# Loading each later head's operand stack in twelve half-length pieces, one every five tiles of keys, instead of in six transfers at once

## The chip, the cores and the metric

The kernel runs on one core of a Trainium2 chip. The metric is the device time of one execution, in microseconds; lower is better. The engines are TensorE (PE, with its weight loads PEld), VectorE (DVE), ScalarE (ACT), GpSimd (POOL) and SyncE (SP). Sixteen DMA engines move data between DRAM and the on-chip memory.

## What is computed

One block of a transformer on 4096 tokens of width 256: half a mixture-of-experts layer, attention, and half a mixture-of-experts layer again, each behind a layer norm. The part that the change touches is the attention:

```python
qkv = jnp.einsum('bsi,oi->bso', x, w_qkv)            # S = 4096 tokens, 16 heads of 16
logits = jnp.einsum('bhsd,bhtd->bhst', q, k) * scale
logits = jnp.where(mask, logits, neg_inf)            # causal
probs = jax.nn.softmax(logits, axis=-1)
out = jnp.einsum('bhst,bhtd->bhsd', probs, v)
```

## The kernel before, in words

**Precision by parts.** Queries and keys are split into three bf16 parts each (the number, its rest, the rest of that). The projections are computed once, the parts are stored to `qk_parts` in DRAM, and every head reads its rows back into a *stack* of 96 partitions by 4096 tokens, once for queries (c = 0) and once for keys (c = 1): `K_PARTS = (3, 2, 1)` says that the first query part stands against three key parts, the second against two, the third against one. Two more partitions hold the row maxima of the queries. There are two stack buffers; head h uses buffer h % 2, so head h + 1 can be loaded once all transposed scores of head h - 1 are done.

**The order of the work.** `attention_steps()` is one list that all engines walk. Its steps are the *tiles* of probabilities: head by head, block of 512 queries by block (j = 0 to 7), tile of 128 keys by tile; a head has 144 tiles. Around them stand, a fixed amount of work ahead (`LEAD`), the scores that only serve to find the row maxima ("scores"), then for each block the joining of its maxima ("unit_max") and their way into the stack ("max_row"), and, up to five tiles behind, the products with the values ("pv").

- PE computes the scores for the maxima (L967 to L971), the transposed scores of a tile (L989) and the products with the values (L932). L940 is the helper that issues the score matmuls in groups of 32 columns. The first scores of the next head stand before tile 98 of this one; they are the first that wait for its stack (`stack_ready`, L914).
- ACT takes the exponential of each tile (L730).
- DVE reduces the scores to maxima (L1344) and copies the joined maxima (L1356).
- POOL zeroes what lies behind the diagonal in the last four tiles of each block (L519, the "select"), splits the joined maxima in two bf16 parts (L510, L512), and issues the stack loads (L484). It does these in the order of the list, each when its turn comes.
- SP sends the row maxima into the stack (L599), two transfers of 1 KB per block.

**The load of a stack** is `load_stack` (L474): six transfers, issued back to back: 48 partitions of queries and 48 of keys (384 KB each), 32 and 32 (256 KB each), 16 and 16 (128 KB each), every partition's row 4096 tokens or 8 KB long. The steps list places the load of head 1 before tile 6 of head 0, and that of head h + 1 before tile 24 of head h. Head 0 is loaded by SP in small blocks and is not changed; head 15 loads nothing, as there is no head 16.

Of the kernel before, what the change touches and what calls it, by code (L numbers as in the profile page):

```python
# [15 lines left out]
S = 4096  # L16
# [3 lines left out]
H = 16  # L20
HD = D // H
# [27 lines left out]
K_PARTS = (3, 2, 1)  # L49
# [12 lines left out]
PV_LAG, PV_PAUSE, FINISH_LAG = 5, 2, 3  # L62
GRID = 32
MAX_ROW_LAG = 4
FIRST_LOAD = 6

UNITS = [(h, j) for h in range(H) for j in range(NJ)]

# [6 lines left out]
PER_HEAD = ITEMS // H  # L75
# [32 lines left out]
def keys_of(j, i, k):  # L108

    if i == DIAGONAL:  # L110
        return 0, QB
    return k * QB, min(QB * j + P * i, (k + 1) * QB)


def attention_steps():

    begun, ended = EARLY_CHUNKS, EARLY_CHUNKS
    for _ in range(NEXT_CHUNKS):
        yield "begin_chunk", begun
        begun += 1  # L120
        if begun - ended > 1:
            yield "end_chunk", ended
            ended += 1
    yield "end_chunk", ended
    ended += 1
    a, a_done, b_done, u, unsent = 0, 0, 0, 0, []
    summed, pause, unfinished = 0, 0, []
    for n in range(ITEMS):
        while a < len(A_ITEMS) and a_done < b_done + LEAD:
            h, j, i, k = A_ITEMS[a]  # L130
            yield "scores", a
            lo, hi = keys_of(j, i, k)
            a_done += hi - lo
            a += 1
            if a == len(A_ITEMS) or A_ITEMS[a][:2] != (h, j):
                yield "unit_max", u
                unsent.append((a + MAX_ROW_LAG, u))
                u += 1
            while unsent and (unsent[0][0] <= a or a == len(A_ITEMS)):
                yield "max_row", unsent.pop(0)[1]  # L140
            if n == 0 and begun < len(CHUNKS):
                if begun > ended:
                    yield "end_chunk", ended
                    ended += 1
                yield "begin_chunk", begun
                begun += 1
            elif ended < begun:
                yield "end_chunk", ended
                ended += 1
        h, j, t = B_ITEMS[n]  # L150
        if n == FIRST_LOAD:
            yield "load_stack", 1
        if j == 3 and t == 0 and 1 <= h < H - 1:
            yield "load_stack", h + 1
        yield "probs", n
        b_done += QB - max(t - TPJ * j, 0) * P

        for _ in range(0 if pause else 2):
            if summed > n - PV_LAG:
                break  # L160
            yield "pv", summed
            h, j, t = B_ITEMS[summed]
            summed += 1
            if t == TPJ * (j + 1) - 1:
                yield "acc", h * NJ + j
                unfinished.append((n + FINISH_LAG, h * NJ + j))
                pause = PV_PAUSE + 1
                break
        pause = max(pause - 1, 0)
        while unfinished and unfinished[0][0] <= n:  # L170
            yield "finish", unfinished.pop(0)[1]
    while summed < ITEMS:
        yield "pv", summed
        summed += 1
    yield "acc", len(UNITS) - 1
    for _, u in unfinished:
        yield "finish", u
    yield "finish", len(UNITS) - 1
# [67 lines left out]
def macaron_block(nc, x_in, w_qkv_t, w_out_t, gate_w, gate_b, w1, w2, w3, bias_cols, out):  # L246
    with ExitStack() as ctx:
        sig = Signals(nc, ctx)
# [21 lines left out]
        parts_dram = nc.dram_tensor("qk_parts", (2, 3, D, S), BF16).ap()  # L270
# [49 lines left out]
        def carve(n):  # L320
            wat[0] += n
            assert wat[0] <= WORK
            return work[:, wat[0] - n:wat[0]]
# [15 lines left out]
        def bf(ap):  # L339
            return ap.bitcast(BF16)  # L340

        wat[0] = 0
        stack = bf(carve(2 * 2 * S // 2)).rearrange("p (b c s) -> p b c s", b=2, c=2)
# [30 lines left out]
        def _(eng):  # L374
            need = Waits(eng)
# [91 lines left out]
            def part3(n):  # L467
                b, b_f = n % SPLIT_BF, n % SPLIT_F
                need.wait_ge(sig.part2, n + 1)
                need.wait_ge(sig.parts_stored[b], 16 * (n // SPLIT_BF))  # L470
                eng.tensor_tensor(split_bf[:, b, 2], split_f[:, b_f], split_bf[:, b, 1],  # L471
                                  ALU.subtract).then_inc(sig.part3, 1)

            def load_stack(h):  # L474
                last = EARLY_CHUNKS if h < H // KD else len(CHUNKS)
                for n in range(last - SPLIT_BF, last):
                    need.wait_ge(sig.parts_stored[n % SPLIT_BF], 16 * (n // SPLIT_BF + 1))
                need.wait_ge(sig.scores_t, PER_HEAD * (h - 1))
                r = 0
                for part, count in enumerate(K_PARTS):  # L480
                    q_rows = parts_dram[0, part, h * HD:(h + 1) * HD, :].unsqueeze(0).to_broadcast([count, HD, S])
                    k_rows = parts_dram[1, 0:count, h * HD:(h + 1) * HD, :]
                    for c, src in enumerate((q_rows, k_rows)):
                        eng.dma_start(stack[r * HD:(r + count) * HD, h % 2, c, :], src).then_inc(sig.stack[h % 2], 16)  # L484
                    r += count

            def attention():
                need.wait_ge(sig.staged[0], len(STAGES))
                eng.memset(v_aug[:, :, :, HD:VW], 1.0).then_inc(sig.ones, 1)
                need.wait_ge(sig.layer[0][2], N_TILES)  # L490
                need.wait_ge(sig.weighted[0], KD * N_TILES)
                need.wait_ge(sig.v_part[0], KD * N_TILES)
                for b in range(2):
                    need.wait_ge(sig.ones, 1 + b)
                    eng.memset(stack[QK_ROWS:QK_ROWS + M_PARTS, b, 1, :], 1.0).then_inc(sig.ones, 1)
                need.wait_ge(sig.ones, 3)
                eng.memset(maxima, NEG).then_inc(sig.ones, 1)
                for n in range(EARLY_CHUNKS):
                    part3(n)
                for what, n in attention_steps():  # L500
                    if what == "end_chunk":
                        part3(n)
                    elif what == "load_stack":
                        load_stack(n)
                    elif what == "unit_max":
                        b = n % MAX_RING
                        need.wait_ge(sig.neg_max, n + 1)

                        need.wait_ge(sig.a_full, row_place[n - MAX_RING] + 1 if n >= MAX_RING else 0)
                        eng.tensor_copy(max_parts[:, b, 0], neg_max[:, b, :]).then_inc(sig.max_parts, 1)  # L510
                        need.wait_ge(sig.max_parts, 2 * n + 1)
                        eng.tensor_tensor(max_parts[:, b, 1], neg_max[:, b, :], max_parts[:, b, 0],  # L512
                                          ALU.subtract).then_inc(sig.max_parts, 1)
                    elif what == "probs":
                        h, j, t = B_ITEMS[n]
                        lo = (t - TPJ * j) * P
                        if lo >= 0:
                            need.wait_ge(sig.exp, n + 1)
                            eng.affine_select(  # L519
                                out=p_ring[:, n % P_RING, lo:lo + P], in_=p_ring[:, n % P_RING, lo:lo + P],  # L520
                                compare_op=ALU.is_ge, fill=0.0, base=0, pattern=[[1, P]], channel_multiplier=-1,
                            ).then_inc(sig.causal, 1)

            route(0)
            tiles(0)
            attention()
            route(1)
            tiles(1)
# [236 lines left out]
        def _(eng):  # L765
            need = Waits(eng)
# [147 lines left out]
            def stack_ready(h, j):  # L914
                if h == 0:
                    for sc in range(j + 1):
                        need.wait_ge(sig.first_stack[sc], 96)
                else:
                    need.wait_ge(sig.stack[h % 2], 96 * ((h + 1) // 2))

            def pv(n):

# [21 lines left out]
            def attention():  # L944
# [4 lines left out]
                for what, n in attention_steps():  # L949
# [5 lines left out]
                    elif what == "scores":  # L955
                        h, j, i, k = A_ITEMS[n]
                        lo, hi = keys_of(j, i, k)
                        place = scores_place[n]
                        out = bank[A_BANKS[place % len(A_BANKS)]]
                        stack_ready(h, j)  # L960
                        need.wait_ge(sig.a_done, place - len(A_BANKS) + 1)
                        need.wait_ge(sig.rest1, EARLY_CHUNKS)
# [474 lines left out]
```

## Time and profile before

| | us |
|---|---|
| median of three runs | 2474.4 |
| lowest, highest | 2459.2, 2475.3 |
| the profiled execution | 2466.8 |
| its span | 2465.1 |

| engine | busy us | share of the span |
|---|---|---|
| PE | 2289.1 | 93% |
| PEld | 1923.7 | 78% |
| DVE | 1915.6 | 78% |
| ACT | 1565.5 | 64% |
| POOL | 476.0 | 19% |

The attention takes the stretch from about 492 to 2078 us of the span. "issue" in a row is time in which an engine waited for nothing that the profile shows. DMA traffic is listed by queue: q0 is what POOL issues, q1 what SP issues, q8 and q14 are of the kind "instruction", which no line of the kernel issues. PEclk is the granted share of TensorE's clock: 1.00 is 2.4 GHz, 0.50 is 1.2 GHz.

### The profile page before, as it was taken

What the parts mean: (1) busy time and instruction counts of PE and PEld (TensorE: products, weight loads), DVE (VectorE), ACT (ScalarE), POOL (GpSimd) and SP (SyncE); (2) the same over time, 40 slices, a digit from 0 to 9 for tenths busy, and PEclk for the clock granted to TensorE, in tenths of its full rate; (3) what the DMA queues carried; (4) which work ended last, traced back from release to release, by engine and by line L of the source; (5) the groups of instructions that cost most, each with busy time, mean ns of one, the idle gap of its engine ahead of it and who ended that gap; (6) DMA issues with size and microseconds to landing.
All of it is one profiled execution on the core that took longest, in us unless ns stands there. A gap on an engine that the chain in (4) does not pass through costs nothing.

```text
span 2465.1 us, 97220 instructions
## 1 busy us (share of the span) xinstructions
PE 2289.1 (93%) x42097; PEld 1923.7 (78%) x42097; DVE 1915.6 (78%) x4310; ACT 1565.5 (64%) x3252; POOL 476.0 (19%) x1133
## 2 busy tenths in 40 slices
PE   6799988889999999999999999999999999779998
PEld 5588865358788888897888878888888786748886
DVE  6755544389898998898999988998989894575554
ACT  2244423448787887787888877887878786224441
POOL 1533211311110111111202101111011110043330
PEclk7799978979999999999999999999999999779997
DMA  6311102410110101101101111011010103031112
GB/s 207 91 45 48 42 1 84 138 37 4 29 19 14 29 4 29 29 4 29 20 13 29 15 17 29 4 29 29 4 29 13 20 4 105 1 106 45 49 45 68
DMA packets 78179, 96.12 MB, mean 39 GB/s; under 512 B 26868, under 2 KB 69624, under 8 KB 74872
## 3 DMA queue, kind: packets, MB, share of 16 engines
q0 software_dynamic: 24768, 44.75, 8.9%
q1 hardware_dynamic: 52016, 44.10, 5.7%
q8 instruction: 331, 5.42, 1.0%
q10 hardware_dynamic: 968, 1.06, 0.1%
q14 instruction: 96, 0.79, 0.1%
HBM read 64.14 MB, written 25.43 MB: 36 GB/s over the span
## 4 chain that ended last, share of the span: by engine, by line
PE 85%; issue 6%; DVE 5%; POOL 1%; DMA 1%; ACT 1%; ACTq 0%; POOLq 0%; DVEq 0%
PE bank L940 42%; PE bank L932 18%; PE bank L842 17%; PE bank L890 2%; PE bank L802 2%; PE bank L853 1%; DVE work L1344 1%; PE bank L1025 1%; POOL phase L471 1%; DVE work L1199 1%; PE bank L781 1%; DVE work L1202 1%; PE bank L860 1%; DMA qk_parts<-phase 0%; ACT feat L638 0%
## 5 line engine op out<-in xcount | busy, mean ns | idle before, releaser
L940 PE MATMUL bank<-work 96*32 96x512 bf16 (+6 forms) x19968 | 1484.8, 353 | 26.0 <-issue 22.2
L730 ACT ACTIVATE feat<-bank 128x512 f32<-128x512 f32 (+3 forms) x2304 | 1256.1, 565 | 312.4 <-PE bank L940 235.1
L1344 DVE TENSOR_REDUCE work<-bank 128x1 f32<-128x512 f32 (+3 forms) x2176 | 1288.9, 637 | 104.7 <-PE bank L940 90.4
L932 PE MATMUL bank<-feat,phase 128*17 128x128 f32 x16896 | 1200.2, 275 | 35.2 <-issue 35.2
L940 PEld LDWEIGHTS bank<-work 96*32 96x32 bf16 (+1 forms) x19968 | 890.0, 97 | 118.6 <-issue 30.7
L932 PEld LDWEIGHTS bank<-feat,phase 128*17 128x17 f32 x16896 | 824.0, 99 | 144.0 <-issue 41.6
L842 PE MATMUL bank<-work 128*128 128x256 f32 x1872 | 435.0, 382 | 3.5 <-issue 2.2
L842 PEld LDWEIGHTS bank<-work 128*128 128x128 f32 x1872 | 340.8, 191 | 53.8 <-issue 12.4
L519 POOL TENSOR_SCALAR_AFFINE_SELECT feat<-feat 128x128 f32<-128x128 f32 x512 | 145.6, 292 | 728.4 <-ACT feat L730 722.5
L1252 DVE COPY work<-phase 128x514 f32 x234 | 100.6, 430 | 189.7 <-ACT work L689 59.3
L458 POOL DMA_INDIRECT work<-token_table,row_no x156 | 148.7, 953 | 282.7 <-DVE work L1266 243.3
L673 ACT ACTIVATE work<-work 128x256 f32<-128x256 f32 x156 | 63.6, 408 | 181.5 <-DVE work L1273 181.5
L510 POOL CAST work<-work 128x4 bf16<-128x4 f32 x128 | 23.8, 186 | 590.3 <-DVE work L1350 590.3
L689 ACT ACTIVATE work<-bank,work 128x256 f32<-128x256 f32 x156 | 65.4, 470 | 87.4 <-PE bank L842 87.4
L1341 DVE TENSOR_REDUCE work<-bank 128x4 f32<-128x512 f32 x128 | 87.8, 686 | 11.8 <-PE bank L940 8.0
L940 PE MATMUL bank<-mask_bf,ident_bf 128*32 128x512 bf16 x512 | 87.1, 383 | 0.1
L1320 DVE TENSOR_TENSOR phase<-bank,phase 128x512 f32<-128x512 f32 x32 | 22.1, 691 | 82.3 <-ACT phase L698 75.5
L679 ACT ACTIVATE work<-bank 128x512 f32<-128x512 f32 x78 | 44.9, 576 | 60.8 <-PE bank L853 60.8
L1304 DVE TENSOR_TENSOR x_res<-x_res,bank 128x512 f32<-128x512 f32 x48 | 32.8, 688 | 57.0 <-PE bank L890 30.3
L1273 DVE SCALAR_TENSOR_TENSOR work<-bank,work 128x256 f32<-128x256 f32 x156 | 67.9, 476 | 11.2 <-PE bank L842 10.9
L940 PE MATMUL bank<-ident,work 128*32 128x68 f32 x1024 | 73.0, 225 | 0.4 <-ACT work L736 0.4
L1282 DVE TENSOR_SCALAR work<-bank,work 128x256 f32<-128x256 f32 x156 | 67.9, 478 | 1.7 <-PE bank L842 1.7
(147 smaller groups left out, 1474.9 us busy)
## 6 DMA issues: line engine op xcount, KB each, us to landing
phase<-in_w SPq DMA_DIRECT2D x12, 1024.0 KB, 12.5
qk_parts<-phase SPq DMA_DIRECT2D x32, 384.0 KB, 2.6
work<-qk_parts POOLq DMA_DIRECT2D x30, 384.0 KB, 2.8
token_table<-rows SPq DMA_DIRECT2D x8, 1056.0 KB, 8.9
work<-qk_parts POOLq DMA_DIRECT2D x30, 256.0 KB, 8.7
x_res<-in_x SPq DMA_DIRECT2D x4, 1024.0 KB, 13.5
work<-work SPq DMA_DIRECT2D x256, 1.0 KB
out<-x_res SPq DMA_DIRECT2D x4, 1024.0 KB, 4.4
```

Of the source, the lines that this page charges most:

```text
L458: eng.indirect_dma_start(out=x_slot[:, j % NXG, u, :], out_offset=None, in_=table[f], in_offset=bass.IndirectOffsetOnAxis(ap=row_no[:, n:n ...
L519: eng.affine_select(out=p_ring[:, n % P_RING, lo:lo + P], in_=p_ring[:, n % P_RING, lo:lo + P], compare_op=ALU.is_ge, fill=0.0, base=0, pa ...
L689: eng.activation(acts[:, 1, j % 2, m], bank[2][:, m * TILE:(m + 1) * TILE], ACT.Relu, bias=staged[:, j % 2, 0, KD * D + m:KD * D + m + 1], ...
L730: eng.activation(p_ring[:, n % P_RING, lo:QB], bank[bk][:, lo:QB], ACT.Exp, scale=HD ** -0.5).then_inc(sig.exp, 1)
L842: mm = eng.matmul(bank[bk][:, m * TILE:(m + 1) * TILE], staged[:, b, l, k * D + m * P:k * D + (m + 1) * P], acts[:, l, b, k], start=(k == ...
L932: mm = eng.matmul(bank[ACC_BANK][GRID * g:GRID * g + VW, 0:P], v_aug[:, t, h, :], p_ring[:, n % P_RING, g * P:(g + 1) * P], start=(t == 0) ...
L940: mm = eng.matmul(out[GRID * g:GRID * (g + 1), width], left[:, GRID * g:GRID * (g + 1)], right, start=start, stop=stop)
L1252: eng.tensor_copy(staged[:, j % 2, l, :], experts[:, bass.ds(expert, 1), l, :].rearrange("p a w -> p (a w)"),).then_inc(sig.staged[f], 1)
L1273: eng.scalar_tensor_tensor(weighted[:, j % 2, m], bank[4][:, m * TILE:(m + 1) * TILE], staged[:, j % 2, 2, KD * D + m:KD * D + m + 1], w_r ...
L1282: eng.tensor_scalar(acts[:, 2, j % 2, m], bank[3][:, m * TILE:(m + 1) * TILE], staged[:, j % 2, 1, KD * D + m:KD * D + m + 1], 0.0, ALU.ad ...
L1341: eng.tensor_reduce(maxima[:, h % 2, j, :, 0], scores[:, 0:QB].rearrange("p (i s) -> p i s", i=TPJ), AX_X, ALU.max).then_inc(sig.a_done, 1)
L1344: eng.tensor_reduce(maxima[:, h % 2, j, i, k + 1:k + 2], scores[:, 0:hi - lo], AX_X, ALU.max).then_inc(sig.a_done, 1)
```

## The change

The six transfers become twelve: each is cut into the tokens 0 to 2047 and 2048 to 4095, so a partition's row is 4 KB. The pieces stand before tiles 24, 29, 34, ... 79 of the head before, also for head 1. The wait before the first scores of a head counts twelve transfers instead of six.

```diff
-FIRST_LOAD = 6
+
+LOAD_PIECES = [(part, c, half) for part in range(len(K_PARTS)) for c in range(2) for half in range(2)]
+LOAD_FIRST, LOAD_EVERY = 24, 5
...
-        if n == FIRST_LOAD:
-            yield "load_stack", 1
-        if j == 3 and t == 0 and 1 <= h < H - 1:
-            yield "load_stack", h + 1
+        piece, between = divmod(n - PER_HEAD * h - LOAD_FIRST, LOAD_EVERY)
+        if h < H - 1 and between == 0 and 0 <= piece < len(LOAD_PIECES):
+            yield "load_stack", (h + 1, piece)
...
-                r = 0
-                for part, count in enumerate(K_PARTS):
-                    q_rows = parts_dram[0, part, h * HD:(h + 1) * HD, :].unsqueeze(0).to_broadcast([count, HD, S])
-                    k_rows = parts_dram[1, 0:count, h * HD:(h + 1) * HD, :]
-                    for c, src in enumerate((q_rows, k_rows)):
-                        eng.dma_start(stack[r * HD:(r + count) * HD, h % 2, c, :], src).then_inc(sig.stack[h % 2], 16)
-                    r += count
+                part, c, half = LOAD_PIECES[piece]
+                count, r = K_PARTS[part], sum(K_PARTS[:part])
+                tokens = slice(half * S // 2, (half + 1) * S // 2)
+                if c == 0:
+                    src = parts_dram[0, part, h * HD:(h + 1) * HD, tokens].unsqueeze(0).to_broadcast([count, HD, S // 2])
+                else:
+                    src = parts_dram[1, 0:count, h * HD:(h + 1) * HD, tokens]
+                eng.dma_start(stack[r * HD:(r + count) * HD, h % 2, c, tokens], src).then_inc(sig.stack[h % 2], 16)
...
-                    need.wait_ge(sig.stack[h % 2], 96 * ((h + 1) // 2))
+                    need.wait_ge(sig.stack[h % 2], 16 * len(LOAD_PIECES) * ((h + 1) // 2))
```

Only POOL's order changes. These are POOL's instructions over one head in the middle of the attention before; `work<-qk_parts` is a stack load, the shape its partitions and tokens, AFFINE_SELECT the select at the diagonal, CAST and TENSOR_TENSOR the splitting of a block's maxima:

```order
L519 AFFINE_SELECT feat<-feat 128x128 x6
L484 DMA work<-qk_parts 48x1x4096 x2
L484 DMA work<-qk_parts 32x1x4096 x2
L484 DMA work<-qk_parts 16x4096 x2
L510 CAST work<-work 128x4
L512 TENSOR_TENSOR work<-work 128x4
L519 AFFINE_SELECT feat<-feat 128x128 x8
L510 CAST work<-work 128x4
L512 TENSOR_TENSOR work<-work 128x4
L519 AFFINE_SELECT feat<-feat 128x128 x4
```

And the same stretch of the changed program (its lines stand two to three further down):

```order
L521 AFFINE_SELECT feat<-feat 128x128 x6
L487 DMA work<-qk_parts 48x1x2048 x3
L512 CAST work<-work 128x4
L514 TENSOR_TENSOR work<-work 128x4
L521 AFFINE_SELECT feat<-feat 128x128 x3
L487 DMA work<-qk_parts 48x1x2048
L521 AFFINE_SELECT feat<-feat 128x128
L487 DMA work<-qk_parts 32x1x2048 x3
L521 AFFINE_SELECT feat<-feat 128x128 x3
L487 DMA work<-qk_parts 32x1x2048
L521 AFFINE_SELECT feat<-feat 128x128
L487 DMA work<-qk_parts 16x2048
```

It goes on with the splitting of the next block's maxima, the last three loads (16x2048 x3), and the four selects of the following block. The twelve loads do not stand alone: three follow each other after tile 23, one and then three stand on the two sides of the select of tile 39, one and one on the two sides of the select of tile 59, and three behind the next maxima.

## Rows read from the trace of the kernel before

**Rows 1.** The page: busy time of PE, and the chain that ended last.
```profile
PE 2289.1 (93%) x42097; PEld 1923.7 (78%) x42097; DVE 1915.6 (78%) x4310; ACT 1565.5 (64%) x3252; POOL 476.0 (19%) x1133
PE 85%; issue 6%; DVE 5%; POOL 1%; DMA 1%; ACT 1%; ACTq 0%; POOLq 0%; DVEq 0%
```

**Rows 2.** Waits of PE: who, for what, us in total, times, longest us.
```profile
PE bank L932 <- issue: 35.2, 9, 5.8
PE bank L940 <- issue: 22.2, 5, 7.8
```

**Rows 3.** The chain in order of time, head 1: start us, us, what.
```profile
636.86 5.83 issue
```

**Rows 4.** DMA queues from 627.0 to 627.3 us: packets, MB, share of 16 engines.
```profile
q8 instruction: 1, 0.02, 20.0%
```

**Rows 5.** DMA queues from 627.3 to 639.8 us.
```profile
DMA packets 807, 1.08 MB, mean 87 GB/s; under 512 B 675, under 2 KB 675, under 8 KB 675
...
q0 software_dynamic: 807, 1.08, 50.0%
```

**Rows 6.** DMA queues from 639.8 to 640.1 us.
```profile
q8 instruction: 1, 0.02, 27.9%
```

**Rows 7.** DMA queues from 630.2 to 645.9 us, one whole load.
```profile
DMA packets 948, 1.62 MB, mean 103 GB/s; under 512 B 753, under 2 KB 753, under 8 KB 753
...
q0 software_dynamic: 945, 1.58, 52.1%
q8 instruction: 2, 0.03, 1.0%
```

**Rows 8.** DMA queues from 1985 to 2060 us, head 15, no load.
```profile
q8 instruction: 15, 0.25, 1.4%
```

**Rows 9.** DMA queues from 632.3 to 639.8 us, the middle of a load.
```profile
DMA packets 158, 0.92 MB, mean 122 GB/s; under 512 B 46, under 2 KB 46, under 8 KB 46
```

**Rows 10.** Stretches: busy us (instructions) by engine, then PEclk, DMA share, GB/s.
```profile
640.00:646.00 6.00, 3.31 (x55) 2.65 (x59) 1.38 (x2) 1.15 (x3) 0.58 (x2) 0.50 0.33 82
...
1319.00:1327.00 8.00, 8.00 (x227) 7.32 (x221) 7.36 (x17) 6.66 (x13) 1.51 (x6) 1.00 0.71 133
2004.00:2012.00 8.00, 8.00 (x228) 7.22 (x222) 7.36 (x16) 6.67 (x13) 1.51 (x6) 1.00 0.02 6
```

**Rows 11.** POOL in order of time at tile 24 of heads 1, 8, 9 and 15.
```profile
628.28 0.54 POOL L519 TENSOR_SCALAR_AFFINE_SELECT feat<-feat 128x128 f32<-128x128 f32 x2 [0.15 <-ACT feat L730]
628.76 3.45 POOL L484 DMA_DIRECT2D work<-qk_parts  x6
...
1315.08 3.45 POOL L484 DMA_DIRECT2D work<-qk_parts  x6
...
1407.63 3.45 POOL L484 DMA_DIRECT2D work<-qk_parts  x6
...
1999.77 0.54 POOL L519 TENSOR_SCALAR_AFFINE_SELECT feat<-feat 128x128 f32<-128x128 f32 x2 [0.15 <-ACT feat L730]
```

**Rows 12.** PE in order of time, head 0, behind the load of head 1.
```profile
531.03 0.63 PE L932 MATMUL bank<-feat,phase 128*17 128x128 f32 x8 [4.56 <-issue]
```

**Rows 13.** POOL in order of time, head 8: selects 38, 39; 57 to 59; two maxima.
```profile
1324.81 0.54 POOL L519 TENSOR_SCALAR_AFFINE_SELECT feat<-feat 128x128 f32<-128x128 f32 x2 [0.15 <-ACT feat L730]
...
1337.05 0.91 POOL L519 TENSOR_SCALAR_AFFINE_SELECT feat<-feat 128x128 f32<-128x128 f32 x3 [0.31 <-ACT feat L730]
1341.62 0.19 POOL L510 CAST work<-work 128x4 bf16<-128x4 f32 x1 [3.67 <-DVE work L1350]
...
1362.47 0.19 POOL L510 CAST work<-work 128x4 bf16<-128x4 f32 x1 [9.08 <-DVE work L1350]
```

**Rows 14.** DVE and ACT, head 8: block 5's maxima copied; its first exponential.
```profile
1326.12 0.27 DVE L1356 CAST work<-bank 8x128 bf16<-8x128 f32 x1
...
1337.76 1.25 ACT L730 ACTIVATE feat<-bank 128x512 f32<-128x512 f32 x2 [0.16 <-PE bank L940]
```

**Rows 15.** DMA queues from 392 to 465 us, rows of 1 KB, issued by SP.
```profile
q1 hardware_dynamic: 7872, 7.47, 31.1%
```

More of the change, by code:

```diff
@@ L472, in part3, with load_stack @@
                                   ALU.subtract).then_inc(sig.part3, 1)
-            def load_stack(h):
+            def load_stack(h, piece):
                 last = EARLY_CHUNKS if h < H // KD else len(CHUNKS)
@@ L503, in attention @@
                     elif what == "load_stack":
-                        load_stack(n)
+                        load_stack(*n)
                     elif what == "unit_max":
```

## The prediction

> **What bounds the kernel now.** I first read the page: PE is busy for 93% of the span and the chain that ended last lies on it for 85%, with 6% of "issue" [rows 1]. So the other engines cost nothing as long as PE is fed. Then the waits of PE: the largest are for no engine but for "issue", 35.2 + 22.2 = 57.4 us in 14 waits of up to 7.8 us [rows 2]. All fourteen lie in the attention, one in each of heads 0 to 14 but head 8. The chain shows the one of head 1: from 636.86 us on PE stands still for 5.83 us [rows 3], 8 us after POOL issued the six loads of head 2's stack at 628.76 [rows 11].
>
> What PE lacks there is told by the queue of the kind "instruction". In head 15, which loads nothing, q8 moves 15 packets in 75 us, one every 5.0 us [rows 8]. In head 1 one starts at about 627.2 [rows 4], then in 12.5 us there is none, only q0, the stack load [rows 5], and the next comes at 639.8 [rows 6]. PE stops 9.7 us after the first of them and goes on at 642.69, 2.9 us after the second. So the program's own instructions were late, behind the stack's data. From this follows the slack: PE lives 9.7 us on a packet and needs the next 2.9 us before it can go on, so a spacing of 6.8 us does no harm, and a packet may be **1.8 us** late against the usual 5.0.
>
> **What it costs now.** Heads 8 and 9 give the length of a head without such a wait: 1407.63 - 1315.08 = 92.55 us from load to load [rows 11]. From the last selects before tile 24 in head 1 (628.28) to the same in head 15 (1999.77) are 1371.5 us, for 14 heads, against 14 x 92.55 = 1295.7. So the loads of heads 1 to 14 cost 75.8 us. That is more than their 57.4 - 4.6 = 52.8 us of waiting (4.56 us is head 0's, [rows 12]), a factor of 1.44: behind the wait the granted clock is 0.50, that is 1.2 GHz [rows 10], and PE, which had stood still, works at half speed for a while. Head 0 at the same factor: 4.56 x 1.44 = 6.6 us. **All loads together: 82.4 us.** The heads with no wait show that this is all of it: head 8's PE is busy for 8.00 us of 8 with the DMA engines at 0.71, like head 15's at 0.02 [rows 10]. The stack's data do not slow PE's work, they only hold up its instructions.
>
> **The change, part by part.**
>
> *Removed: the burst of 1.57 MB.* Minus 82.4 us, if nothing takes its place.
>
> *Added: the pieces, which are not evenly spaced.* POOL issues a piece as soon as it gets to it, and waits only at selects and maxima. By its order the three pieces of tiles 24, 29 and 34 go out together after select 23 (at 1315.1 in head 8); those of tiles 39 to 54 together around select 39, ten us later (select 38 and 39 start at 1324.81); those of 59 and 64 at about 1338; the last three behind the maxima at 1341.6 [rows 13]. The first burst is 3 x 192 KB = 0.59 MB. The second is 192 + 3 x 128 KB, again 0.59 MB. The third and fourth have 0.20 MB each.
>
> *What a burst does to the instruction packets.* The load of head 2 moves 1.58 MB in 15.7 us [rows 7] and holds the packet back until 639.8, 9.6 us after the data began to flow. For a burst of 0.59 MB there are three readings. In proportion (9.6/15.7 of the time that 0.59 MB takes at 103 GB/s, 5.7 us) the hold is 3.5 us. At the rate of the load's middle, 122 GB/s [rows 9], the burst is gone after 4.8 us. At worst the packet comes with the burst's last byte at the mean rate, 5.7 us. At best packets get through and the hold is under 1.8 us. I take 4.8 us, since in a burst three transfers of nearly one size run side by side to the end, as in the middle of the load.
>
> *The residual.* A packet is due every 5.0 us, at any moment of the burst, and stalls PE by what it is late over 1.8 us. Not every packet lies in the way: a hold of 9.6 us should cost 9.6 - 2.5 - 1.8 = 5.3 us on average, and the fifteen loads cost 57.4/15 = 3.8, so 0.72 of the packets are caught. A burst with a hold T costs 0.72 x (T - 1.8)^2 / (2 x 5.0): for 4.8 us 0.65, for 3.5 us 0.21, for 5.7 us 1.1. Fifteen loads have 30 large bursts: **19 us** (6 and 33 at the ends; none at best). The two small bursts of each head are drained in 0.20 MB / 103 GB/s = 1.9 us and cost nothing. So short a wait should not lower the clock: I take no factor.
>
> The Trainium skill (DMA: Bandwidth & Descriptors, "Why a DMA increments its semaphore by 16 and not by 1") says that a transfer issued by POOL runs on the largest number of engines up to 16 that divides the slowest dimension on both sides. By it the pieces with three and two copies run on three and two engines, a large burst puts 16 packets of 4 KB on each of nine engines, and with half of the load's 0.68 us a packet (below) a packet is held 5.4 us and the residual would be an estimate of 22 us instead of 19. The trace agrees roughly: by the rule ten of sixteen engines, 0.63, carry the middle of a load, and the share there is 0.71.
>
> *POOL's own time.* Six issues take 3.45 us [rows 11], so twelve take 6.9, or 0.58 each. POOL is busy for 19% of the span and waits before nearly every select. The piece before tile 39 puts 0.6 us ahead of the select of tile 39, the one before 59 the same; the product that waits for the select stands five tiles behind, about 3 us. Nothing.
>
> *The row maxima.* SP's transfer of block 5's maxima now falls into the second burst: they are copied at 1326.12 in head 8 and first used for an exponential at 1337.76, 11.6 us later [rows 14]. A hold of 5.7 us fits. Nothing, but see the last rival.
>
> *Being in time.* The last pieces go out from 1341.6 to 1343.4 and are there by 1346; the next head's first scores come just before the maxima at 1362.5 [rows 13]. Some 16 us of slack. Head 1's load, moved from tile 6 to 24, has the same slack. More packets of half the size: by time per byte they cost the same. SP's rows of 1 KB took 0.311 x 73 x 16 / 7872 = 0.046 us each [rows 15], the stack's packets of 8 KB (948 less 753 small ones and 3 of instructions, 192) 0.521 x 15.7 x 16 / 192 = 0.68 us [rows 7], so a packet's time goes with its bytes.
>
> **The sum** on the profiled execution: 2466.8 - 82.4 + 19 = 2403. That execution lies 0.3% under the median of 2474.4 and inside the three runs. Since the waits depend on how packets and loads fall together, I take part of that spread to be theirs and leave the sum as it is: **2403 us**, 2.9% under the median.
>
> **The rivals.**
>
> 1. *As summed, short waits left:* 2390 to 2417 between the two ends of the hold. Chance 0.68.
> 2. *No waits left at all.* For it: packets got through head 8's load with no harm. Against: the slack is 1.8 us and a large burst lasts 4.8. Then 2466.8 - 82.4 = 2384, just below it. Chance 0.17.
> 3. *The bursts hold the packets longer than their own drain,* up to 7.5 us, as the pieces of one burst queue up behind each other: 0.72 x 5.7^2 / 10 = 2.3 us a burst, 70 us: 2454 at the far end, about 2435 for half of that. Chance 0.06.
> 4. *The wait of PE is not the loads' doing and stays.* The Trainium skill (Runtime: NRT & Kernel Launch, "Instruction fetch mechanics") has PE hold 2048 instructions, and says that fetching is mostly hidden. If PE stopped for something else near tile 36, the change would do nothing: 2467 to 2475. Against: PE ran dry 9.7 us after a packet [rows 3, 4], there is none between [rows 5], and head 15 has no wait. Here the measurement decides. Chance 0.06.
> 5. *Slower: a 4 KB packet takes as long as one of 8 KB.* Then a large burst, with as many packets in its busiest engines as the whole load, holds the instructions for the same 9.6 us, and there are two in each head. 30 x 3.8 = 114 us of waiting, times 1.44 = 164: 2384 + 164 = 2548; with the row maxima held as long, up to 1 us more a head. It turns slower where a burst costs over 82.4/30 = 2.7 us. Against: time goes with bytes [rows 7, 15]. Chance 0.03.
>
> **Range and chances.** A measurement of this kernel can hardly tell less than 1%, 25 us, from nothing. Below 2450: rivals 1, 2 and most of 3, 0.91. Within 1%: rival 4, 0.06. Slower: 0.03. The range goes from 2382 (no waits, with 2 us for the other stretches) to 2430, which takes in the upper bound of the residual and a part of rival 3.
>
> **What would show it.** The "issue" waits of PE in the attention fall from 57 us to some 20 or less, none over 4 us. In the undisturbed parts of a head the distance from one load to the next is 92.55 us as before, and the mean comes near 94. Queue q8 has no gap over 8 us. The half-clock stretch behind tile 40 is gone in most heads. I would be wrong if waits of 4 us and more stood behind the second burst, at tile 40 or later, if PE waited at the first scores of a head, or if the time per head were longer while "issue" is short.

## The result, and the profile after

| | before | changed |
|---|---|---|
| median, us | 2474.0 | 2401.8 |
| lowest, highest | 2459.2, 2475.3 | 2391.0, 2408.2 |
| the profiled execution | 2466.8 | 2391.0 |

The ratio is 0.9719, with a 95% interval of 0.9677 to 0.9761: faster by 2.8%. The forecast was 2403 us. The profiled execution is the shortest of the four. In a second series, on another chip, the changed kernel had a median of 2406.3 us (ratio 0.9768, 0.9732 to 0.9804).

The page of the changed kernel, its busy times and its chain, against [rows 1]:

```profile
PE 2263.3 (95%) x42097; PEld 1910.2 (80%) x42097; DVE 1912.2 (80%) x4310; ACT 1568.1 (66%) x3252; POOL 525.6 (22%) x1223
...
PE 87%; DVE 5%; issue 4%; POOL 1%; DMA 1%; ACT 1%; ACTq 0%; POOLq 0%; DVEq 0%
```

PE has as many instructions as before; POOL's ninety more are the added pieces. PE's waits for "issue", against [rows 2] (L934 and L942 are L932 and L940 of before; the columns are the total, times and longest):

```profile
PE bank L934 <- issue: 3.0, 2, 1.6
PE bank L844 <- issue: 2.9, 5, 1.0
PE bank L942 <- issue: 1.4, 2, 0.8
```

Of 57.4 us in fourteen waits, 4.4 us in four are left in the attention; L844 is in the expert layers. Of the 4% of "issue" that the chain still has, almost all lies ahead of the attention (17.0% of the chain there, 0.5% inside). One of the four, in head 3, in the chain of waits:

```profile
827.64 1.49 issue
```

It has the same anatomy as before, only shorter. The DMA queues from 817.5 to 817.9 us hold one instruction packet, those from 817.9 to 826.5 none, those from 826.5 to 826.9 the next:

```profile
q8 instruction: 1, 0.02, 15.0%
...
DMA packets 1103, 0.60 MB, mean 69 GB/s; under 512 B 959, under 2 KB 959, under 8 KB 1103
...
q0 software_dynamic: 1087, 0.59, 28.8%
...
q8 instruction: 1, 0.02, 16.1%
```

That is a gap of about 9.0 us between the two packets where 5.0 are usual [rows 8], against 12.6 in head 1 of before [rows 4 to 6], with the second burst's 0.59 MB in between. Before each of the other three waits the trace has such a gap too, of 8.4, 8.1 and 8.7 us; two of the four stand behind the first burst of a head and two behind the second. Behind the wait of head 3 PE has its full clock (the value before the DMA share, 1.00, that is 2.4 GHz), where [rows 10] had 0.50 behind a long one:

```profile
829.00:835.00 6.00, 5.86 (x149) 4.90 (x151) 4.89 (x8) 4.42 (x9) 2.16 (x6) 1.00 0.09 19
```

POOL in order of time in head 8, where [rows 13] had only selects and maxima; L487 are the pieces:

```profile
1274.66 1.84 POOL L487 DMA_DIRECT2D work<-qk_parts  x3
...
1284.62 0.65 POOL L487 DMA_DIRECT2D work<-qk_parts  x1
1285.28 0.31 POOL L521 TENSOR_SCALAR_AFFINE_SELECT feat<-feat 128x128 f32<-128x128 f32 x1
1285.52 1.80 POOL L487 DMA_DIRECT2D work<-qk_parts  x3
...
1297.13 0.60 POOL L487 DMA_DIRECT2D work<-qk_parts  x1
1297.74 0.31 POOL L521 TENSOR_SCALAR_AFFINE_SELECT feat<-feat 128x128 f32<-128x128 f32 x1
1297.98 0.51 POOL L487 DMA_DIRECT2D work<-qk_parts  x1
...
1301.61 1.51 POOL L487 DMA_DIRECT2D work<-qk_parts  x3
```

There are the four bursts. At tile 24 of head 9 the next begins, so a head without a wait takes 1367.22 - 1274.66 = 92.56 us, as before [rows 11]:

```profile
1367.22 1.86 POOL L487 DMA_DIRECT2D work<-qk_parts  x3
```

The cleanest measure of what the loads cost is the stretch from the first to the last exponential, since nothing outside the attention enters. This is ACT's exponential line: duration min/median/max in ns, first and last start in us; before, changed, and the later kernel with twelve transfers of 16 partitions spaced out, which has no issue waits in the attention (e5 below):

```profile
L730 ACT ACTIVATE feat<-bank x2304: 272/597/922, 513.9 to 2070.5; 128x512 f32<-128x512 f32 x192
...
L732 ACT ACTIVATE feat<-bank x2304: 273/598/927, 515.4 to 1994.5; 128x512 f32<-128x512 f32 x192
...
L729 ACT ACTIVATE feat<-bank x2304: 271/597/902, 513.8 to 1987.2; 128x512 f32<-128x512 f32 x192
```

1556.6, 1479.1 and 1473.4 us. So the loads cost 83.2 us before and 5.7 after the change. The same stretch for every profile but e3's ("12 of 16" are twelve transfers of 16 partitions each):

| kernel | transfers per head, how placed | stretch, us | median of runs, us | ratio to before (95%) |
|---|---|---|---|---|
| before | 6, at once | 1556.6 | 2474.0 | |
| changed | 12 halves, tiles 24 to 79 | 1479.1 | 2401.8 | 0.9719 (0.9677-0.9761) |
| changed, again | the same | 1480.4 | 2406.3 | 0.9768 (0.9732-0.9804) |
| e1 | as changed, nearly no bytes | 1474.8 | 2392.7 | 0.9712 (0.9644-0.9781) |
| e2 | 12 halves, at once | 1554.1 | 2483.2 | 1.0086 (1.0046-1.0126) |
| e3 | 6 whole, tiles 24 to 74 | | 2417.8 | 0.9814 (0.9738-0.9891) |
| e4 | 12 of 16 neighbours, at once | 1548.8 | 2469.2 | 1.0030 (0.9991-1.0068) |
| e5 | 12 of 16 neighbours, spaced | 1473.4 | 2392.9 | 0.9696 (0.9662-0.9730) |
| e6 | 12 of 16 spread, at once | 1474.2 | 2392.5 | 0.9712 (0.9678-0.9745) |
| e7 | 6, copies innermost, at once | 1545.4 | 2463.4 | 0.9999 (0.9967-1.0030) |
| e8 | 6, copies innermost, spaced | 1478.7 | 2396.9 | 0.9708 (0.9663-0.9752) |
| e9 | 12 of 16 spread, spaced | 1473.5 | 2395.2 | 0.9725 (0.9691-0.9758) |
| e10 | before, every load twice | 1594.0 | 2521.6 | 1.0244 (1.0184-1.0304) |
| e11 | as changed, truly one by one | 1476.2 | 2397.0 | 0.9726 (0.9686-0.9766) |

(Of e3's four runs the longest, 2447.9 us, is counted as a slow one and left out, and with it the profile, which is of that run. Ratios are to runs of the kernel before on the same chip, so two kernels of different series are best compared by them. A stretch is that of one execution: where a kernel waits much, its executions differ, those of before from 2443 to 2483 us, so that 1545 and 1557 say little about each other.)

### The profile page after: what moved, and what is told of

The parts are those of the page before. It is cut to its first block, busy times and chain, and to the rows that moved or that the text cites. A ratio compares the mean times of both kernels' runs of the same rounds, so it can differ in the third digit from the quotient of the medians.

```text
span 2389.3 us, 97310 instructions
## 1 busy us (share of the span) xinstructions
PE 2263.3 (95%) x42097; PEld 1910.2 (80%) x42097; DVE 1912.2 (80%) x4310; ACT 1568.1 (66%) x3252; POOL 525.6 (22%) x1223
## 4 chain that ended last, share of the span: by engine, by line
PE 87%; DVE 5%; issue 4%; POOL 1%; DMA 1%; ACT 1%; ACTq 0%; POOLq 0%; DVEq 0%
PE bank L942 43%; PE bank L934 18%; PE bank L844 17%; PE bank L804 2%; PE bank L892 2%; PE bank L855 1%; PE bank L1027 1%; POOL phase L472 1%; DVE work L1201 1%; PE bank L783 1%; DVE work L1346 1%; DVE work L1204 1%; PE bank L862 1%; DMA qk_parts<-phase 1%; ACT feat L640 0%
## 5 line engine op out<-in xcount | busy, mean ns | idle before, releaser
L942 PE MATMUL bank<-work 96*32 96x512 bf16 (+6 forms) x19968 | 1463.3, 350 | 5.3 <-DVE work L1346 3.7
L1346 DVE TENSOR_REDUCE work<-bank 128x1 f32<-128x512 f32 (+3 forms) x2176 | 1286.5, 637 | 37.4 <-PE bank L942 27.7
L934 PE MATMUL bank<-feat,phase 128*17 128x128 f32 x16896 | 1188.3, 272 | 3.0 <-issue 3.0
L942 PEld LDWEIGHTS bank<-work 96*32 96x32 bf16 (+1 forms) x19968 | 879.4, 96 | 91.5 <-DVE work L1346 15.6
L934 PEld LDWEIGHTS bank<-feat,phase 128*17 128x17 f32 x16896 | 808.0, 98 | 107.5 <-issue 3.9
L844 PE MATMUL bank<-work 128*128 128x256 f32 x1872 | 435.1, 382 | 3.5 <-issue 2.9
L844 PEld LDWEIGHTS bank<-work 128*128 128x128 f32 x1872 | 340.5, 191 | 54.1 <-issue 12.6
L487 POOL DMA_DIRECT2D work<-qk_parts x180 | 103.7, 580 | 5.4 <-issue 3.7
L942 PE MATMUL bank<-mask_bf,ident_bf 128*32 128x512 bf16 x512 | 87.0, 382 | 0.1
L1275 DVE SCALAR_TENSOR_TENSOR work<-bank,work 128x256 f32<-128x256 f32 x156 | 67.8, 476 | 11.2 <-PE bank L844 10.9
L1306 DVE TENSOR_TENSOR x_res<-x_res,bank 128x512 f32<-128x512 f32 x48 | 32.8, 688 | 54.0 <-PE bank L892 27.2
L942 PE MATMUL bank<-ident,work 128*32 128x68 f32 x1024 | 71.9, 226 | 0.4 <-ACT work L738 0.4
```

Source lines behind the costliest of these rows:

```text
L487: eng.dma_start(stack[r * HD:(r + count) * HD, h % 2, c, tokens], src).then_inc(sig.stack[h % 2], 16)
L844: mm = eng.matmul(bank[bk][:, m * TILE:(m + 1) * TILE], staged[:, b, l, k * D + m * P:k * D + (m + 1) * P], acts[:, l, b, k], start=(k == ...
L934: mm = eng.matmul(bank[ACC_BANK][GRID * g:GRID * g + VW, 0:P], v_aug[:, t, h, :], p_ring[:, n % P_RING, g * P:(g + 1) * P], start=(t == 0) ...
L942: mm = eng.matmul(out[GRID * g:GRID * (g + 1), width], left[:, GRID * g:GRID * (g + 1)], right, start=start, stop=stop)
L1275: eng.scalar_tensor_tensor(weighted[:, j % 2, m], bank[4][:, m * TILE:(m + 1) * TILE], staged[:, j % 2, 2, KD * D + m:KD * D + m + 1], w_r ...
L1346: eng.tensor_reduce(maxima[:, h % 2, j, i, k + 1:k + 2], scores[:, 0:hi - lo], AX_X, ALU.max).then_inc(sig.a_done, 1)
```

## The experiments

**Is it the bytes at all?** e1 keeps every transfer of the changed kernel and takes away, from head 2 on, nearly all that it carries. The edit:

```diff
-                tokens = slice(half * S // 2, (half + 1) * S // 2)
+                width = S // 2 if h < 2 else 64
+                tokens = slice(half * S // 2, half * S // 2 + width)
```

> Leaves out nearly all of the data: from head 2 on each of the twelve pieces carries 64 tokens instead of 2048 (the stack keeps older rows, so the output is not the reference's). The number of transfers, their places and POOL's work are those of the changed kernel. Theory (instruction packets held up by the stack's bytes): no 'issue' waits of PE from head 1 on, time near the floor of 2384 us, so 2380 to 2398. Rival (issuing the pieces on POOL, or their number, costs something by itself): no faster than the changed kernel, 2398 to 2408.

2392.7 us, no issue wait in the attention. Issuing twelve pieces costs nothing that can be seen; of what is left in the changed kernel, 4 to 6 us are the bytes' by the stretch (1479.1 and 1480.4 against 1474.8). The medians are 9 us apart, but come from different chips, and the ratios to before hardly differ. It also shows the floor.

**Load more.** e10 is the kernel before, with each stack loaded a second time before tile 60 (shown in part; the waits for a stack count twelve transfers):

```diff
+        if j == 5 and t == 0 and h < H - 1:
+            yield "load_stack_again", h + 1
...
+                    elif what == "load_stack_again":
+                        need.wait_ge(sig.stack[n % 2], 192 * ((n + 1) // 2) - 96)
+                        load_stack(n)
```

> The kernel before, with every stack of heads 1 to 15 loaded a second time, the same six transfers at once, before tile 60 of the head before. Theory (each burst of 1.57 MB costs PE 3.8 us of missing instructions, 5.5 with the clock): 15 new bursts cost 55 to 90 us, 2520 to 2560, with new 'issue' waits of 3 to 8 us behind tile 60. Rival (PE's waits belong to the place near tile 36 and not to the load): no new waits, 2460 to 2480.

2521.6 us, 52 us above the same series' median before of 2469.8, a little under the expected cost of 55 to 90, and inside the range of times. Two pieces of its chain in head 7, behind the two loads that POOL issues at 1241.19 and 1270.02 us:

```profile
1250.33 6.36 issue
...
1279.20 6.77 issue
```

The second load has its own wait, 9.2 us behind its issue, far from tile 36. Eleven of the fifteen second loads have one. The place is not the cause, the load is. The added loads cost less than the first ones: by the stretch 37.4 us (1594.0 - 1556.6), 2.5 us each against 5.5, and 27 issue waits of 79.1 us together against fourteen of 57.4. Why is not shown. There is also a wait that before does not have, for the small transfers that bring the row maxima into the stack:

```profile
PE bank L945 <- DMA work<-work: 5.4, 2, 4.5
```

**Size or spacing?** The change does two things. e2 has its halves, all at tile 24:

```diff
-        piece, between = divmod(n - PER_HEAD * h - LOAD_FIRST, LOAD_EVERY)
-        if h < H - 1 and between == 0 and 0 <= piece < len(LOAD_PIECES):
-            yield "load_stack", (h + 1, piece)
+        if h < H - 1 and n - PER_HEAD * h == LOAD_FIRST:
+            for piece in range(len(LOAD_PIECES)):
+                yield "load_stack", (h + 1, piece)
```

> The size alone: twelve half-length transfers, all at tile 24. Theory A (what counts is all the data in flight at once, 1.57 MB as before): the instruction packet is held about 9.6 us as before, time 2460 to 2480. Theory B (a packet waits only for the sixteen rows of one transfer that stand before it on its DMA engine, now half as long): holds of 3 to 5 us, time 2395 to 2425.

2483.2 us, just above the range of theory A: no gain, and by the ratio a loss of 0.5 to 1.3%. The profiled execution (2474.3 us, the second shortest of ten) does not show where the loss lies. Its waits of PE for issue in the attention:

```profile
PE bank L934 <- issue: 36.1, 8, 8.0
PE bank L942 <- issue: 14.9, 5, 5.2
...
PE bank L980 <- issue: 2.5, 1, 2.5
```

e3 has the spacing, with the six whole transfers (shown in part; the transfers have their full length again):

```diff
-LOAD_PIECES = [(part, c, half) for part in range(len(K_PARTS)) for c in range(2) for half in range(2)]
-LOAD_FIRST, LOAD_EVERY = 24, 5
+LOAD_PIECES = [(part, c) for part in range(len(K_PARTS)) for c in range(2)]
+LOAD_FIRST, LOAD_EVERY = 24, 10
```

> The spacing alone: the six whole transfers before tiles 24, 34, 44, 54, 64, 74. By POOL's order they go out as 0.79 MB, then 0.52 MB around tile 40, then 0.26 MB in two. Theory A (data in flight): holds of 6.4 us and 4.3 us, residual 15 x 0.72 x (4.6^2 + 2.5^2)/10 = 30 us, so 2405 to 2425. Theory B (sixteen rows of 8 KB of one transfer): rows half to fully as slow as before, holds of 5.4 to 9 us, so 2425 to 2460.

2417.8 us (2407.5 to 2425.5 in three runs). Against 2469.1 of the same series spacing alone gives 46 to 51 us, by the ratio and by the medians, some two thirds of the gain. Halving alone gives nothing; that halving on top of spacing gives the rest is likely but thin, since e3's interval (0.9738 to 0.9891) overlaps both of the changed kernel's. It went as theory A says in e2; in e3 the runs stand in theory A's range and at the border of theory B's, which decides little.

**Which work stands in the way?** e4 sends all bytes at once, but in twelve transfers of 16 neighbouring partitions, each row 8 KB long (shown in part; all twelve stand before tile 24):

```diff
+                row, c = LOAD_PIECES[piece]
+                q_part, k_part = STACK_ROWS[row]
+                src = parts_dram[c, k_part if c else q_part, h * HD:(h + 1) * HD, :]
+                eng.dma_start(stack[row * HD:(row + 1) * HD, h % 2, c, :], src).then_inc(sig.stack[h % 2], 16)
```

> All bytes at once at tile 24, but as twelve transfers of 16 partitions with rows of 8 KB, instead of 48, 32 and 16 partitions. Theory A (data in flight): the load is held only by its total, so waits of several us stay unless the load is drained much faster; at the 103 GB/s of before 2460 to 2480. Theory B (the wide transfers run on two or three DMA engines each and put sixteen rows in a row on each; one of 16 partitions puts one row on each of sixteen engines): the load drains in 5 to 8 us instead of 15.7 and hardly holds any instruction packet, 2384 to 2400, so at least as fast as the changed kernel.

2469.2 us, no gain. Theory B, that it was the long run of rows on a few DMA engines, fell: now all sixteen are busy, and every one of the fifteen loads stalls PE. One load of e4, from 1120.1 to 1133.6 us:

```profile
DMA packets 401, 1.60 MB, mean 119 GB/s; under 512 B 207, under 2 KB 207, under 8 KB 207
...
q0 software_dynamic: 383, 1.57, 89.8%
```

Each row takes 0.898 x 13.5 x 16 / 192 = 1.01 us (the small packets counted in), while POOL, which issues all twelve in 5.8 us, has the next transfer out after half of that. So rows must pile up. The question became why they are so slow.

**The memory side.** e6 differs from e4 in one index: a transfer writes partitions r, r + 6, ... r + 90 instead of neighbours (a reordering of the contraction, alike for queries and keys).

```diff
-                eng.dma_start(stack[row * HD:(row + 1) * HD, h % 2, c, :], src).then_inc(sig.stack[h % 2], 16)
+                eng.dma_start(stack[row:QK_ROWS:len(STACK_ROWS), h % 2, c, :], src).then_inc(sig.stack[h % 2], 16)
```

> As the kernel with twelve transfers of 16 partitions at once at tile 24, but each transfer writes partitions r, r+6, ... r+90 instead of 16 neighbours (the same rows in another order, alike for queries and keys). Theory P (the load drains at 105 to 116 GB/s because all engines write neighbouring partitions at one time): it drains in 4 to 7 us instead of 13.5, a packet is held 5 us at most, residual at most 15 x 3.2^2/10 = 15 us over the kernel without bytes (2393): 2392 to 2412. Theory Q (the limit is the reading side or POOL's queue): still 13.5 us, 2460 to 2475.

2392.5 us, at the floor, with everything at once and no issue wait in the attention. One load, from 1093.7 to 1101.2 us, and POOL's issues for it:

```profile
DMA packets 385, 1.60 MB, mean 213 GB/s; under 512 B 191, under 2 KB 191, under 8 KB 191
...
q0 software_dynamic: 383, 1.57, 78.3%
q8 instruction: 1, 0.02, 1.1%
```

```profile
1092.51 5.76 POOL L484 DMA_DIRECT2D work<-qk_parts  x12
```

213 GB/s instead of 119, 0.49 us a row, and POOL issues one transfer of sixteen rows every 0.48 us. The rows are gone as fast as they come, and no gap between instruction packets behind a load is over 6.8 us. Theory P held. The Trainium skill (SBUF — State Buffer, "Door 1: The DMA port swizzle") says that the DMA side reaches the memory by sixteen ports, of which 16 neighbouring partitions cover four at 27.2 GB/s each: 109 GB/s by the page. The 119 measured lie somewhat above it; that rows laid further apart go faster agrees with the page.

e7 goes between: the six transfers of before with the copies innermost, so that more engines work on more partitions at once (shown in part; no halves, all six before tile 24).

```diff
+                if c == 0:
+                    src = parts_dram[0, part, h * HD:(h + 1) * HD, :].unsqueeze(1).to_broadcast([HD, count, S])
+                else:
+                    src = parts_dram[1, 0:count, h * HD:(h + 1) * HD, :].rearrange("k d s -> d k s")
```

> The six whole transfers at once at tile 24, with the partitions of a transfer ordered by dimension first and copy second. Theory P: sixteen engines write 48 (or 32) partitions at a time instead of 16, so the load drains in 7 to 10 us; half of the 82 us of waiting stays: 2415 to 2455. Theory Q: drained in 13.5 us or more, 2460 to 2480.

2463.4 us: no gain, though the load drains as theory P says, in under 10 us. I was wrong about what that is worth. The queues from 924.8 to 934.5 us, and from 934.5 to 935:

```profile
DMA packets 281, 1.54 MB, mean 159 GB/s; under 512 B 93, under 2 KB 93, under 8 KB 93
...
q0 software_dynamic: 281, 1.54, 91.7%
...
q8 instruction: 1, 0.02, 16.0%
```

POOL has issued all six after 3.0 us, and the instruction packet comes only with the last of them, as late after the load's start as before (9.7 against 9.6 us). It is not the time that the load takes that counts, and not its bytes, but what is already queued on the DMA engines when the packet falls due. An estimate from these rows, for an even spread of the 192 rows over sixteen engines, twelve each: in e7 a row takes 0.917 x 9.7 x 16 / 188 = 0.76 us, so four have gone when the last is issued and eight are left, 6.1 us of work; in e4 six are left of 1.01 us, 6.3 us of work; in e6 about one. The lateness of the packets is of that size: 5.9 us here and 6.1 in the load of e4 above (gaps of 10.9 and 11.1 us where 5.0 are usual), and at most 7.1 and 6.7 in the fifteen loads of each, as it depends on when in the load a packet falls due.

**The same, spaced out.** If that is so, neighbours do no harm when they are issued no faster than they drain. e5 is e4 at the changed kernel's places:

> Twelve transfers of 16 neighbouring partitions, rows of 8 KB, before tiles 24, 29, ... 79: at the changed kernel's places. Theory (an instruction packet waits for what is already queued on its own DMA engine): the largest burst is four such rows per engine, issued 0.58 us apart and 1.0 us each, so never more than 2 to 3 us queued, against 16 rows of 4 KB on each of nine engines in the changed kernel: hardly a wait, 2388 to 2400. Rival (only the spread over partitions helped in the run with partitions r, r+6, ...; neighbours stay slow): as the changed kernel, 2400 to 2412.

2392.9 us, the floor, and no issue wait in the attention. A burst has at most four rows per engine, of 1 us at most. Its stretch is 5.7 to 7.0 us shorter than the changed kernel's, with the same number of transfers at the same places and the same bytes; what differs is how the rows are spread, so this points to the sixteen rows that a half puts on a few engines. e8 is e7 spaced, before tiles 24, 34, ... 74:

> Six whole transfers, copies innermost so that each runs on all sixteen engines with two or three rows of 8 KB, before tiles 24, 34, ... 74. Bursts of two transfers queue six rows of 0.73 us, 4.4 us, less what drains while they are issued: holds up to 4 us on every engine. Theory (queued work): short waits only, 2395 to 2412, under the six whole transfers on two or three engines each (2422). Rival (it is bytes per burst alone that counts): as those, 2415 to 2430.

2396.9 us, against 2417.8 for the same six transfers with the copies outermost (on another chip; ratios 0.9708 and 0.9814): the same bytes per burst, so it is not bytes alone. Its trace has four short waits, all behind the first burst, the largest: six rows per engine. e9 is e6 spaced:

> The twelve transfers of 16 spread partitions, placed before tiles 24, 29, ... 79 as in the changed kernel. Theory P: no burst lasts over 2 us, no instruction packet is held over its slack, time that of the kernel without bytes: 2386 to 2400. Theory Q: bursts of 0.39 and 0.52 MB take 3.4 and 4.6 us as neighbours would, a residual of 10 to 20 us: 2400 to 2415.

2395.2 us, like e6.

**The bunching.** e11 makes POOL wait for the exponential before each piece's own tile:

```diff
+                need.wait_ge(sig.exp, PER_HEAD * (h - 1) + LOAD_FIRST + LOAD_EVERY * piece)
                 part, c, half = LOAD_PIECES[piece]
```

> The changed kernel, with POOL made to wait for the exponential before each piece's own tile, so that the twelve pieces really go out one every five tiles (some 3 us apart). Theory (what remains in the changed kernel are bursts of three and four pieces): one piece puts 16 rows of 4 KB on two or three DMA engines, under 4 us of work and on few engines, so most of the rest goes: 2390 to 2401. Rival (each piece's own sixteen rows are enough to hold a packet): as the changed kernel or above, 2400 to 2412.

2397.0 us, inside the range: of the 5.7 to 7.0 us that the loads still cost in the attention, 2.8 are left, and of four or five issue waits two. (e1 and e6, with no wait, lie up to 1.4 us above e5 themselves, so "half" is rough.) The changed kernel once more, beside e6, e7 and e9:

> The changed kernel once more, beside these three on one chip: 2392 to 2410, and in the trace two to six short 'issue' waits of PE behind tiles 24 and 40.

2406.3 us (2396.5 to 2410.0), with five short issue waits. All six runs of e6 (2388.2 to 2395.7) lie under all six of it: **e6 beats both kernels**, by 0.6% over the changed one by the medians, 6 us of it in the attention. e5 has the same floor, but the changed kernel was not run on its chip; its ratio lies clear under that of this series and not under that of the first.

## Why the prediction was right, point by point

- *What PE lacked.* Held. Less data (e1), more data (e10) and the same data out of the way (e5, e6) move the waits, and each wait that is left in the changed kernel's attention has a late packet of q8. Rival 4, that the fetching is hidden and the wait something else's, is out.
- *82.4 us for all loads.* Held: 83.2 by the stretch of the exponentials, whose floor was seen only later. Its part, PE's half-speed stretch behind a long wait, shows in the same ratio: 83.2 us lost for 57.4 us of waiting. Behind the short wait looked at the clock stayed full, as was taken.
- *No long wait left, POOL's issues free, row maxima and last pieces in time.* Held: the longest wait is 1.6 us, there is no other new wait of PE, and e1 has the same issues at the floor. The mean head takes 92.95 us from first exponential to first exponential, better than the 94 forecast. One sign failed: q8 was to have no gap over 8 us, and has four, of 8.1 to 9.0.
- *The bunching.* Held, burst by burst. Unbunched (e11), about half of the rest goes.
- *The residual, 19 us.* **Mis-sized.** In the profiled executions it is 5.7 and 7.0 us (1480.4 - 1473.4); the medians give 9 over e1, on another chip, and 14 beside e6, but they hold what differs outside the attention too. The step that failed is the choice of the sizes that go into a burst's cost, a hold of 4.8 us with a slack of 1.8. They give 13 waits of up to 3.0 us; there were four and five, the longest 1.6. In head 3 the packet was 9.0 - 5.0 = 4.0 us late and PE waited 1.5, so the slack was 2.5 there (1.8 to 2.9 behind the four). A hold of 4.0 with a slack of 2.5 gives 30 x 0.72 x 1.5^2 / 10 = 4.9 us, near the 5.7; the reading "in proportion", 3.5 us, had given 6. How much of the error is the hold's and how much the slack's four waits do not tell. A burst of the changed kernel does last longer than I took, 6.8 us, but its transfers start one after another, and it seems that on one DMA engine only the rows of one of them are queued. An estimate from the trace from 1276 to 1282.8 us in head 8 of the changed kernel: 137 packets of 4 KB (686 less 546 small and 3 of instructions) take 0.476 x 6.8 x 16 / 137 = 0.38 us each with the small ones counted in, in a slow burst; from 819.7 to 826.7 in head 3 144 take 0.27 us. Sixteen of these are 4.3 to 6 us, and a packet that falls due in the midst of them would wait for the rest alone.

```profile
DMA packets 686, 0.60 MB, mean 89 GB/s; under 512 B 546, under 2 KB 546, under 8 KB 683
...
q0 software_dynamic: 683, 0.56, 47.6%
...
q0 software_dynamic: 972, 0.59, 34.6%
```

- *How 2403 still met 2401.8.* Two errors cancelled, and that is luck. The floor was taken from one profiled execution: 2466.8 - 82.4 = 2384. The kernels without waits in the attention (e1, e5, e6, e9) have medians of 2392.5 to 2395.2. The profiled execution of before had come early to the attention (its first exponential starts at 513.9 us; in the fourteen profiles it lies between 513.8 and 523.3), and what follows the last exponential was short too (394.6 us, against 397.4 to 399.1 in these four). From the median, 2474.0 - 82 = 2392 and a residual of 6 would have given 2398, and 4 to 8 us of the two measured medians would stay open. The forecast's sizes were 8 us too low in one term and 5 to 13 too high in the other.
- *Two sums of the prediction.* Half of rival 3's 70 us gives 2384 + 35 = 2419, not 2435. The second estimate of the residual, 22 us, comes out only with 9/16 in place of the 0.72; with 0.72 a hold of 5.4 us gives 28. Neither enters the forecast.
- *Which part of the change works.* I had costed the burst by its bytes. The direction was right; but e7 and e8 show that bytes are only the stand-in for what is queued on the engines, and e2 that halving by itself does not help and is slightly slower; that its added transfers land on engines that were free is a guess. The second estimate of the residual, by the number of engines that a transfer uses, was no better.

## What to carry to other kernels

An engine that works through many small instructions, as PE does here, lives on a stream of instruction packets (one every 5.0 us), and queued data hold them up. Look for waits on nothing ("issue") behind large transfers, and at the gaps in the queue of the kind "instruction". Then do not only cut bytes or seconds, but what is queued at one time: give all engines few rows each, try a transfer's partitions apart, and issue no faster than it drains. All this was seen in one kernel, with loads that POOL issues; whether loads from another queue hold the packets as well was not tried.

## What was not expected

- The order in which the same rows are laid out in the on-chip memory decides the rate of a load: 119 GB/s into 16 neighbouring partitions at a time, 213 GB/s into every sixth, at the same source, sizes and queue.
- In e7 the load drains sooner (159 GB/s instead of 103), and the instruction packet of 16 KB still comes 9.7 us behind the load's start, as before, and the kernel is no faster (0.9999).
- The time from the start to the first exponential differs by up to 9.5 us from execution to execution, with no edit there. What differs there was not looked into.
- That the packets queue on the same DMA engine as the rows is concluded from the rates and the lateness of the packets (e4 to e8); the trace does not name the engine of a packet, so neither this nor how the rows are spread over the engines was seen directly.
